# Edges sorted on chip into 32-slot cells in the first graph layer, and a second layer that gathers and sums over the cells by one-hot products

## What is computed

```python
h = node_feat @ W_emb + b_emb
norm = _edge_norm(etype, dst, h.dtype)
for l in range(L):
    W = jnp.einsum('rb,bdf->rdf', w_coe[l], bases[l])
    T = jnp.einsum('nd,rdf->rnf', h, W)
    msg = T[etype, src] * norm
    agg = jax.ops.segment_sum(msg, dst, num_segments=N)
    h = agg + h @ self_loop[l]
    ...  # batch norm and relu
```

## Time and profile before

| | us |
|---|---|
| median of 3 runs (6409.76 to 6421.92) | 6416.69 |
| the profiled execution | 6414.97 |
| its span | 6412.9 |
| PE / DVE / POOL / ACT busy | 4024.7 / 3905.0 / 3985.6 / 1444.4 |

### The profile page before, as it was taken

One profiled execution on the slowest core, in us unless ns is written; L12 is line 12 of the kernel. 1 busy time (PEld: TensorE's weight loads), 2 busy tenths in 40 slices (PEclk: granted clock), 3 DMA queues, 4 the chain that ended last, 5 costly groups with the idle time before them and its releaser, 6 DMA issues. The chain is left out here.

```text
span 6412.9 us, 94832 instructions
## 1 busy us (share of the span) xinstructions
PE 4024.7 (63%) x21143; PEld 3018.8 (47%) x21144; DVE 3905.0 (61%) x6685; ACT 1444.4 (23%) x2058; POOL 3985.6 (62%) x3707
## 2 busy tenths in 40 slices
PE   6477677777777774545454544445497466666788
PEld 2244444444444443444444444444353366666777
DVE  7689898998989983222222222222312699999933
ACT  3122222222222221111111111111100355555600
POOL 0377777777777775777777777777600177777600
PEclk9799999999999996565656555655598788878899
DMA  5355555555555555555555555555495334434288
GB/s 207 115 162 147 165 152 155 162 146 164 152 155 162 147 163 161 165 165 162 165 163 165 163 164 164 165 162 166 136 315 178 125 145 156 159 145 158 90 273 258
DMA packets 845320, 1061.63 MB, mean 166 GB/s; under 512 B 302559, under 2 KB 750153, under 8 KB 832074
## 3 DMA queue, kind: packets, MB, share of 16 engines
q1 hardware_dynamic: 613226, 547.26, 28.3%
q0 software_dynamic: 109760, 225.01, 13.3%
q10 hardware_dynamic: 122272, 288.74, 11.9%
HBM read 762.45 MB, written 298.11 MB: 165 GB/s over the span
## 5 line engine op out<-in xcount | busy, mean ns | idle before, releaser
L572 POOL DMA_INDIRECT rows<-table,recs x3430 | 3248.6, 947 | 1300.2 <-issue 1202.5
L607 PE MATMUL acc<-rows,hot 128*128 128x264 f32 (+1 forms) x6860 | 1696.1, 413 | 1325.9 <-DMA rows<-table,recs 910.0
L607 PEld LDWEIGHTS acc<-rows,hot 128*128 128x128 f32 x6860 | 1360.0, 254 | 1635.8 <-DVE hot L731 721.3
L746 DVE TENSOR_TENSOR wkey<-count_up,key 128x1176 f16<-128x1176 f16 x784 | 1077.0, 1374 | 0.0
L1070 POOL TENSOR_TENSOR a_weights<-a_powers,a_counts 128x896 f32<-128x896 f16 x245 | 721.4, 2950 | 334.4 <-ACT a_powers L1160 309.3
L738 DVE TENSOR_SCALAR pen<-state_and_spare 128x896 bf16<-128x896 f16 x343 | 141.9, 414 | 1246.8 <-ACT state_and_spare L650 1246.8
L1120 PE MATMUL a_psum<-state_and_spare,a_weights 128*128 (+1 forms) x4802 | 660.4, 308 | 297.5 <-DVE a_weights L1238 152.9
L1120 PEld LDWEIGHTS a_psum<-state_and_spare,a_weights 128*128 128x128 f32 x4802 | 650.2, 224 | 310.6 <-issue 212.0
L650 ACT ACTIVATE state_and_spare<-tps 128x896 f16<-128x896 f16 x343 | 314.5, 917 | 1863.6 <-PE tps L597 1828.3
L661 ACT ACTIVATE state_and_spare<-wps 128x392 f32 x784 | 389.2, 497 | 1423.4 <-PE wps L615 1418.6
L615 PE MATMUL wps<-wkey,whot 128*128 128x392 f16 x2352 | 518.6, 332 | 245.6 <-DVE wkey L746 241.7
(11 more groups left out here) (171 smaller groups left out, 2538.1 us busy)
## 6 DMA issues: line engine op xcount, KB each, us to landing
rows<-in_edge_attr SPq DMA_DIRECT2D x343, 320.0 KB, 4.5
counts_by_source_f<-state_and_spare ACTq DMA_DIRECT2D x49, 1568.0 KB
csr<-counts_by_source_f SPq DMA_DIRECT2D x343, 224.0 KB, 2.6
counts_by_destination_f<-state_and_spare ACTq DMA_DIRECT2D x343, 224.0 KB, 2.4
no_edge_penalty<-pen ACTq DMA_DIRECT2D x343, 224.0 KB, 2.9
s_ring<-counts_by_destination_f SPq DMA_DIRECT2D x98, 784.0 KB, 4.4
a_pen<-no_edge_penalty SPq DMA_DIRECT2D x49, 1568.0 KB, 9.9
a_counts<-counts_by_source_f SPq DMA_DIRECT2D x49, 1568.0 KB, 6.7
```

The lines of the kernel that those rows point to most:

```text
L572: e.indirect_dma_start(out=rows[:, j, 0:D], out_offset=None, in_=k.table_d[l], in_offset=bass.IndirectOffsetOnAxis(ap=recs[:, j, 4:5].bitc ...
L607: m = e.matmul(acc[:, 0:gw], hot[:, j, :], rows[:, j, :], start=j == 0, stop=j == SLOTS - 1)
L746: e.tensor_tensor(wkey[:, q % 4, :, :], repeat(count_up[:, 0:WC], WSLOTS), spread(key[:, s], WC), ALU.is_equal).then_inc(whot_made, 1)
```

## The change

The two calls of phase_layer stay in the program, but run only if a value computed on the chip (k.most) says so; otherwise phase_first and phase_second run in their place. k.most asks for the old way when a quarter of a tile (32 targets) spans more than 20 chunks of 64 edges, a tile more than 70, or when more than 32 edges of a quarter are left over.

phase_first keeps the gathers and the float32 products of the first layer. Its counting is new. A quarter's edges lie in 10 columns of 128. By source tile and quarter they form cells; each cell gets a column of 32 slots. PE computes the rank of each edge in its cell with products by an earlier-than matrix (rank_quarter), edges over 32 go to a second column of the own tile (OWN) or to a column for leftovers (LEFT), and PE puts source and target of each edge at its slot (place). The counts then are products over cells: for each source tile and quarter a one-hot of sources [32 slots, 128] by a one-hot of targets [32 slots, 32] (count, four blocks of 16, 16, 16 and 1 source tiles). The layer's output h stays in SBUF; no table for layer 1 is written.

phase_second has no gather from DRAM but one column for the leftovers of each tile. For each target tile it takes 51 columns of slots in 13 batches. gather: a one-hot of the slots' sources by the source tile's rows h, split into two float16 halves (256 columns). ACT copies that to grow. scatter: for each column, half and quarter, grow[32 slots, 128] by a one-hot of relation and target [32 slots, 256], added up in four PSUM banks (zps), one for each quarter. transform: eight products with the relations' weights. The turning of counts stays, between the batches. SP loads the sources of the slots, spread over all partitions (five pieces of 320 KB a tile).

phase_prepare finds windows of 32 targets (2 passes and not 8 over the chunk bounds).

```diff
@@ -36,8 +36,21 @@
...
-WGROUPS = 7
-WPG = NW // WGROUPS
+QUARTERS, QW, QCOLS = 4, 32, 10
+QUADS = QUARTERS * QCOLS
+QCHUNKS = QCOLS * P // CHUNK
+NQ = NT * QUARTERS
+QGROUPS = 2
+QPG = NQ // QGROUPS
+CELLS = NT + 2
+OWN, LEFT = NT, NT + 1
+BANK = 512 // QW
+BLOCKS = [(b * BANK, min(BANK, NT - b * BANK)) for b in range(-(-NT // BANK))]
+BATCH = 4
+BATCHES = [range(b, min(b + BATCH, CELLS)) for b in range(0, CELLS, BATCH)]
...
+                k.own8 = narrow("eight_times_tile", [P, NT])
...
+                renew(nc, k)
+                phase_first(nc, k)
+                renew(nc, k)
+                phase_second(nc, k)
+                renew(nc, k)
+            k.attr = inner("attr_sum", [P, NT, D])
...
+            def rank_quarter(t, u):
+                e.wait_ge(cells_made, t + 1)
+                e.wait_ge(rank_used, t * QUARTERS + u)
+                if u == 0:
+                    e.wait_ge(key_out, t * 2)
+                hits = by_cell[:, u * QCOLS:(u + 1) * QCOLS, :]
+                e.matmul(sort[:, 0:QCOLS * NT], k.tri16[:, :], hits.rearrange("p a j -> p (a j)"), start=True, stop=False)
+                for c in range(QCOLS - 1):
+                    n = QCOLS - 1 - c
+                    m = e.matmul(sort[:, (c + 1) * NT:QCOLS * NT].rearrange("p (a j) -> p a j", j=NT), k.ones16[:, :],
+                                 repeat(hits[:, c, :], n), start=False, stop=n == 1)
+                m.then_inc(ranked, 1)
...
+            def count(t, b):
+                lo, n = BLOCKS[b]
+                e.wait_ge(shot_made, t * (len(BLOCKS) + 1) + (b + 2))
+                e.wait_ge(cnt_moved, (t * len(BLOCKS) + b) * QUARTERS)
+                for i in range(2):
+                    for u in range(QUARTERS):
+                        q = slice(u * QW, (u + 1) * QW)
+                        e.matmul(cnt[:, u, 0:n * QW], shotx[q, i, :], xhot[q, i, lo * QW:(lo + n) * QW],
+                                 start=i == 0, stop=False)
+                for j in range(n):
+                    for u in range(QUARTERS):
+                        q = slice(u * QW, (u + 1) * QW)
+                        m = e.matmul(cnt[:, u, j * QW:(j + 1) * QW], shot[q, b % 2, j, :], dhot[q, lo + j, :],
+                                     start=False, stop=j == n - 1)
+                m.then_inc(counted, 1)
+            with e.Fori(0, NT) as t:
+                for g in range(GROUPS):
+                    e.wait_ge(gathered[g], (t + 1) * (16 * PER))
+                    e.wait_ge(hot_made, t * GROUPS + (g + 1))
+                    e.wait_ge(attr_in[g], (t + 1) * 16)
+                    if g == 0:
+                        e.wait_ge(acc_free, t)
+                    for j in range(g * PER, (g + 1) * PER):
+                        m = e.matmul(acc[:, 0:GW], hot[:, j, :], rows[:, j, :], start=j == 0, stop=j == SLOTS - 1)
+                    m.then_inc(ring, 1)
+                    if g < QUARTERS:
+                        rank_quarter(t, g)
+                    if g == QUARTERS:
+                        rank_left(t)
+                place(t)
+                e.wait_ge(h_made, t + 1)
+                e.wait_ge(t_sb, t)
+                e.transpose(pm[:, 0:P], h[:, :], k.ident[:, :]).then_inc(ht_ps, 1)
+                e.wait_ge(key_moved, t + 1)
+                for x in range(3):
...
+                m.then_inc(key_ps, 1)
...
+            e.wait_ge(last_made, 1)
+            e.wait_ge(key_out, NT * 2)
+            for i in range(2):
...
+            m.then_inc(last_ps, 1)
+            e.wait_ge(scale_made, 1)
+            e.matmul(pm[:, 0:1], one_row[:, :], lastv[:, 1:2], start=True, stop=True).then_inc(scale_ps, 1)
...
+                e.activation(key_t[0:CELLS + 1, :, :].rearrange("c x (u r) -> c u x r", r=QW),
+                             sort[0:CELLS + 1, 0:QUARTERS * 3 * QW].rearrange("c (u x r) -> c u x r", u=QUARTERS, x=3),
+                             ACT.Copy).then_inc(key_moved, 1)
...
+                             bias=k.minus1[:, 0:1]).then_inc(key_out, 1)
...
+                e.wait_ge(stored, t * 16)
+                for b, (lo, n) in enumerate(BLOCKS):
+                    e.wait_ge(counted, t * len(BLOCKS) + (b + 3))
+                    for u in range(QUARTERS):
+                        e.activation(mine[:, lo:lo + n, u * QW:(u + 1) * QW],
+                                     cnt[:, u, 0:n * QW].rearrange("p (j d) -> p j d", d=QW), ACT.Copy).then_inc(cnt_moved, 1)
+                e.wait_ge(cnt_moved, (t + 1) * (len(BLOCKS) * QUARTERS))
+                e.dma_start(k.cs_d[False][bass.ds(t, 1), :, :].rearrange("a p c -> (a p) c"),
...
+            def keys(t):
...
+                e.tensor_tensor(dhot[:, :, :], repeat(count_up[:, 0:QW], NT), spread(kd[:, 0:NT], QW), ALU.is_equal)
+                for i in range(2):
+                    e.tensor_scalar(xhot[:, i, :], k.count16[:, :], extra[:, i:i + 1], None, ALU.is_equal)
+                e.tensor_tensor(shotx[:, :, :], repeat(count_up[:, 0:P], 2), spread(key[:, 1, OWN:LEFT + 1], P), ALU.is_equal)\
+                 .then_inc(shot_made, 1)
+                for b, (lo, n) in enumerate(BLOCKS):
+                    e.wait_ge(counted, t * len(BLOCKS) + (b + 1))
+                    e.tensor_tensor(shot[:, b % 2, 0:n, :], repeat(count_up[:, 0:P], n), spread(key[:, 1, lo:lo + n], P),
+                                    ALU.is_equal).then_inc(shot_made, 1)
...
+                        find_left(t)
+                    if g == QUARTERS + 1:
+                        columns(t)
+                        rows_of_slots(t)
+                close(t)
+                keys(t)
+            e.drain()
+            e.reduce_max(last[:, 0:1], most_left[:, :], AX.X)
...
+                def scatter(t, b):
+                    e.wait_ge(g_sb, t * NB + (b + 1))
+                    e.wait_ge(o_made, t * NB + (b + 1))
+                    if b == LASTB:
+                        e.wait_ge(left_in, (t + 1) * 16)
+                    if b == 0:
+                        e.wait_ge(z_sb, t)
+                    for i, c in enumerate(BATCHES[b]):
+                        for q in range(2):
+                            for u in range(QUARTERS):
+                                s = slice(u * QW, (u + 1) * QW)
+                                m = e.matmul(zps[:, u, 0:RELATIONS * QW], grow[s, gslot(b), i, q * D:(q + 1) * D],
+                                             ohot[s, oslot(b), i, :], start=c == 0 and q == 0, stop=c == LEFT and q == 1)
+                    m.then_inc(scattered, 1)
+                def turn_counts(t, g):
...
+                    e.wait_ge(z_sb, t + 1)
+                    e.wait_ge(agg_free, t)
+                    for r in range(RELATIONS):
+                        m = e.matmul(agg[:, 0:D], zsb[:, r, :], k.wr[:, 1, r * D:(r + 1) * D],
+                                     start=r == 0, stop=r == RELATIONS - 1)
+                    m.then_inc(agg_ps, 1)
+                e.wait_ge(hl_made, NSEG)
+                with e.Fori(0, NT) as t:
+                    gather(t, 0)
+                    for b in range(1, NB):
+                        gather(t, b)
+                        scatter(t, b - 1)
+                        if b in TURN_AT:
+                            turn_counts(t, TURN_AT[b])
+                    scatter(t, LASTB)
+                    transform(t)
+            only(e, k, False, run)
...
+                        n = len([c for c in BATCHES[b] if c != LEFT])
+                        e.activation(grow[:, gslot(b), 0:n, :], gps[:, :, :].rearrange("p a (i f) -> p (a i) f", i=2)[:, 0:n, :],
+                                     ACT.Copy).then_inc(g_sb, 1)
+                        if TURN_AT.get(b) in BY_ACT:
```

1153 lines of the change are left out of this document (868 added, 285 removed).

## The result

The changed kernel takes 6489.7 us (median of 4 executions, 6484.7 to 6496.1) where the kernel before takes 6417.1 (4 executions, 6409.8 to 6421.9): a ratio of 1.0115, 95% interval 1.0097 to 1.0132. It is slower by 72.6 us. The forecast was 6915 us, 498 us slower: the sign was right and the size was not. The profiled execution after has a span of 6494.3 us against 6412.9, so 81.4 us are to be found in the traces.

What follows compares the result with a forecast made beforehand. POOL's 35 gathers, 45 us a tile, were taken to bound both layers, with DVE also at the limit in the first. 6415 - 549 (second layer) + 1068 (first) - 19 (preparation and seams) = 6915 us, range 6330 to 7650.

Steps and rivals of the forecast that it cites:

- break-even: Sum of both layers' tile periods at which the change neither gains nor loses: forecast 89.8 us.
- steps 1 to 7: One first-layer tile as a serial chain across engines: 52.5 us + 3P, 66.8 with P and clock, said as 67.
- Step 7: First layer's counts: three blocks, each with four ACT copies behind it, then a short block: 3P + 7.9 us.
- P: PE's time for one block of counts, 8 products of 512 and 64 of 32 columns: 2.8 us, bounds 2.2 and 5.3.
- The clock term: First layer: PE partly at 1.2 GHz after idle stretches, adding 2.1 + 2.8 and about 1 us a tile.
- the seven batches with a turn: Second-layer batches that also transpose counts: 2.4 us each, against 1.9 for the six without.
- no overlap: Rival: products of the four quarters start 109 ns apart; tiles of 62 and 72 us, 8581 us in all; chance 0.07.
- Rival two: The quarters' weight loads follow each other 56 ns apart; second-layer tile 40 us, first-layer 73, 7552 us; chance 0.16.
- The lower bound of 30 us: Second-layer tile's shortest forecast period, with scatter products 27 ns apart; the forecast itself was 33 us.
- Preparation and seams: Outside the tiles: -19 us, from earlier first-layer start -19, window loads -16, second layer's start +9, barriers and branches +7.
- Faster: Rival: neighbouring tiles' steps overlap more, or P and ranks are cheap; 47 and 31 us a tile, 5837 us; chance 0.17.
- The old way: Rival: k.most asks for both old layers, over 4400 us on top, more than 10,000 us in all; chance 0.02.

Runs made afterwards that it cites:

- e5: Changed kernel with the first layer's one-hots made one group earlier, all seven before find_left: 6161.8 us, ratio 0.9608 to the kernel before.
- e8: Changed kernel with e5's order, ranks first, next tile's first two group sums between count blocks, keys' transposes ahead of h's: 5848.2 us, ratio 0.9124 to the kernel before.
- e3: Changed kernel without 60 of the 64 products of 32 columns in a block of counts (counts incomplete): 6405.9 us.
- e4: Changed kernel plus products that nobody reads where PE is idle in the first layer: 6260.1 us, ratio 0.9750 to the kernel before.
- e6: Changed kernel with DVE copying all seven turned segments of the second layer and ACT none: 6449.6 us, ratio 1.0059 to the kernel before.
- e7: Changed kernel without the low halves' products of the second layer's scatter, 204 of 408 in a tile: 6385.4 us.
- e1: Changed kernel with the second layer's scatter loops swapped, all products of one quarter before the next quarter's: 8245.6 us.

## Why the prediction was right in sign and wrong in size

**What bounds the kernel before and the signs: right; the break-even, 88.7 us for 89.8, nearly.** The floor of POOL's gathers left the second layer and stayed in the first; the second gained, the first lost, and the loss was larger.

**First layer, steps 1 to 7.** From the tile shown above, forecast and measured:

| step | forecast us | measured us |
|---|---|---|
| 1 four groups and ranks | 13.6, and 1 for the clock | 16.9 (3061.53 to 3078.45) |
| 2 DVE from last rank to seventh group | 15.9 | 16.0 (to 3094.49) |
| 3 seventh group | 2.2 + 2.1 | 4.2 (to 3098.67) |
| 4 close | 4.3 | 3.6 (to 3102.31) |
| 5 transposes, copies | 1.8 | 1.5 (to 3103.79) |
| 6 keys | 6.8 | 6.9 (to 3110.69) |
| 7 counts | 3 x 2.8 + 7.9, and 2.8 for the clock: 19.1 | 12.3 (to 3123.02) |
| sum | 66.8 | 61.5 |

Steps 2 to 6, which carry the argument that a tile is one chain, are right within 1 us each, and e5 and e8 show that it is the chain and no engine's work: 6.7 and 13.3 us a tile go by another order of the same operations. **Step 7 failed, and in it the term P.** I priced a product of 32 columns like one of 256 columns, at 35 ns with a lower bound of 27, by rows of which none had so few columns. They take 9 to 11 ns each (0.72 us for 64; e3: 9.3 ns): four, one in each quarter, start every 27 to 33 ns for the most part. P was forecast as 2.8 us at full clock and is 1.1 there (1758.01 to 1759.11 in e4); after, at 1.2 GHz (clock 0.50 in the blocks), it is 1.85 in the first block and 1.6 in the others. The forecast's 3P and its 2.8 us of clock make 11.2, measured are 5.1: 6.1 of the 6.8 us. The rest is ACT's four copies, 2.06 us in place of 2.3 with latency. Against it, step 1 is 2.3 us longer than forecast: I left its first group at full clock, and it takes 4.74 us in place of 2.47.

**The clock term: near in sum by luck, wrong in its places.** Forecast 5.9 us a tile (2.1 in step 3, 2.8 in step 7, 1 in step 1); e4 gets 4.7 back. But the 2.8 us were put on the first block, and e4 gets 0.6 in all of step 7 (the eight wide products go from 0.82 to 0.45 us, and the small ones are nearly the same at either clock). Step 1 bears 2.7 instead of 1, by its first group (4.74 for 2.46 us) and the first rank behind it. The sixth group is cold too (4.06 us), but stands in no chain. The clock of the whole first layer is 0.72, under 0.9 as said.

**Second layer: the seven batches with a turn failed.** Twelve distances between gathers and the end of a tile make up the period:

| part | forecast us | measured us |
|---|---|---|
| six batches without a turn | 6 x 1.9 = 11.4 | 11.3 (1.71 to 2.25 each) |
| six batches with a turn | 6 x 2.4 = 14.4 | 11.6 (1.92 or 1.93 each) |
| ACT's own turns, beside these | 0.9 | inside these |
| last batch, with a turn | 2.4 | 1.8 (4002.86 to 4004.65) |
| last scatter, zps, eight products | 3.8 | 3.85 (4004.65 to 4008.50) |
| sum | 32.9 | 28.5 (mean period 28.7) |

The end is right. The six batches without a turn come out right by luck: four take 1.71 to 1.79 us where 1.9 was forecast, and two take 2.25 and 2.08, because ACT, which had just turned a segment, copies late. In a batch with a turn PE does not wait, so its work adds up alone: 0.55 + 0.98 + 0.40 = 1.93 us. The forecast had 0.44 for the gathers, 1.12 for the scatter, 0.6 for the turn, of which 0.2 is a latency that nobody waits for, and 0.2 more, by which it went from 1.7 to 1.9 us a batch without a reason; meant between copy and gather, it is not on the path either when PE is the pace. Two latencies, 0.4 us a batch, are the larger part; the price of a product (35 for 27 ns, 0.14 us with what the change of form costs) is the smaller, 1.0 us of the 4.2 in a tile. ACT's turns cost 0.85 us a tile (e6), but they do so inside distances that the forecast had priced already. That e7 takes only 2.2 us off shows the other limit, ACT's copy, right behind. The mechanism the forecast leaned on, quarters side by side, is shown twice: by the starts (four within 11 ns, the next four 109 ns later), and by e1, in which the same 32 products take 2.41 us at full clock in place of 1.05. That e1's 64.3 us lie near the bound of 62 for no overlap is chance: its quarters overlap in part, and its clock is 0.64. Rival two, loads one after another at 56 ns, falls: a load has 93 ns in the records and 32 of them take 0.77 us. The lower bound of 30 us was no bound, since it kept both latencies.

The forecast weighed a rule of the Trainium skill here ("TensorE: Matmul & The Clock Gate", section "Part 3: Packing small matmuls": four tiles of 32 rows give 3.07 times the speed). By it a tile's scatter takes 14.5 us, an estimate. This case shows four in the time of one, 109 / 27 = 4.0 times, 11.1 us a tile, with a weight load before each product (109 ns is the distance of single products of 256 columns: in e4, 44 of them take 4.97 us and 14 take 1.70). The measurement decides.

**Preparation and seams: the sum failed, by 54 us.** Forecast -19, measured +35, in five places. The first tile's hits start at 218.4 us and not at 205, since the last table store of the preparation comes at 204.6 (196.8 before) and the four window loads take until 218: -6. The 16 us for the window loads were counted twice: they lie inside the period of 45.2, whose first start stands ahead of them. From the first layer's last tile to the second's first it is 105.3 us, a period and 43.6 us, where before it was 2463.8 - 2393.7, a period and 24.9: +19, where 9 and most of 7 had been forecast. The last tile of the second layer is done (the root for its norm starts at 4694.7, before at 4629.9) 4.9 us after its period, which before was 0.6 inside it: +5.5. The next stage's first operation comes 6.9 us after the last one here, and 0.6 before:
```profile
4702.35 6.69 DVE L1647 TENSOR_TENSOR state_and_spare<-state_and_spare,rstd 128x6272 f32<-128x6272 f32 x1
4715.89 1.09 DVE L114 TENSOR_SCALAR s_parts<-state_and_spare  x1 [6.85 <-PEq L212]
```
That is +6, at the place of the branches around the old phases; no run took them out, so their part is not shown. Last, the attention stage, which the change leaves alone, is 8.4 us longer in this execution: its 49 custom operations are busy for 379.0 us and 369.7 before. In the other runs of this study the same operations have 365.2 to 377.3, so I count this as scatter between executions. 2 us stay without a place.

**Small slips in its sums.** The two one-hots xhot are put at 1.0 us in all, while 0.7 ns an element would make 2.2; they take 1.16. With P at 5.3 us and 5.9 of clock the rival without overlap comes to 74 us a tile in the first layer and not 72. In step 7 the terms beside 3P make 3 x 2.3 + 0.7 = 7.6 us and not 7.9; only this touches the forecast, by 15 us.

**The rivals.** Faster: did not happen as the change stands, though by 1.7 us a tile only; of its two conditions ("The steps of neighbouring tiles overlap more than I think, or P and the ranks are cheap") P was cheap. e8 makes the other half true by hand and lands at 5848, beside the 5837 us that the rival gave; that they are so close is luck, since the rival had 47 and 31 us a tile and e8 has 48.4 and 28.7. No overlap: did not happen; four quarters overlap in full, and e1 still overlaps in part. The old way did not run.
